# One PSUM bank in place of two for the scores whose maxima are taken, a fourth bank in the ring of the others, and a new order table

## The reference, cut to what matters

```python
# block 1 (L0), per window; block 2 (L1) adds rel_h and rel_w to the scores before the softmax
h = layer_norm(x, ln1_g, ln1_b)                  # then padded and cut into windows of 14 x 14
q, k, v = heads(h @ w_qkv.T + b_qkv)             # L0: q, k = rotated(q, k)
attn = softmax((q * hd ** -0.5) @ k.T)           # 12 heads
x = x + gamma_1 * ((attn @ v) @ w_proj.T + b_proj)
h = layer_norm(x, ln2_g, ln2_b)
x = x + gamma_2 * (gelu(h @ w_fc1.T + b_fc1) @ w_fc2.T + b_fc2)
```

## Time and profile before

| | |
|---|---|
| median of 3 runs | 572.3 us (570.03 to 575.05) |
| the profiled execution | 571.97 us, span 569.8 us from its first to its last instruction |
| PE busy | 521.0 us, 91% of the span |
| DVE busy | 386.6 us, 68% |
| ACT busy | 367.7 us, 65% |
| POOL busy | 226.7 us, 40% |
| mean granted clock of TensorE | 0.962 of full |

### The profile page before, as it was taken

One profiled execution on the slowest core, in us unless ns is written; L12 is line 12 of the kernel. 1 busy time (PEld: TensorE's weight loads), 2 busy tenths in 40 slices (PEclk: granted clock), 3 DMA queues, 4 the chain that ended last, 5 costly groups with the idle time before them and its releaser, 6 DMA issues.

```text
span 569.8 us, 13552 instructions
## 1 busy us (share of the span) xinstructions
PE 521.0 (91%) x4832; PEld 467.3 (82%) x4832; DVE 386.6 (68%) x915; ACT 367.7 (65%) x778; POOL 226.7 (40%) x324
## 2 busy tenths in 40 slices
PE   8767979999899999999999999999999999979875
PEld 7756868799798988888979898888889898868664
DVE  3887699968987758866758678776858677351230
ACT  0442347653959485969687886969688787755501
POOL 8233427625418353334536253343627234030210
PEclk9896699998999999999999999999999999988899
DMA  7410005000000000000000000000000000000000
GB/s 193 115 41 1 3 2 148 2 1 2 3 1 3 2 2 2 3 2 2 2 3 2 12 22 24 4 1 16 4 3 15 1 17 3 16 3 24 6 14 14
DMA packets 11055, 10.44 MB, mean 18 GB/s; under 512 B 3664, under 2 KB 9456, under 8 KB 10992
## 3 DMA queue, kind: packets, MB, share of 16 engines
q1 hardware_dynamic: 9264, 6.79, 4.5%
q10 hardware_dynamic: 1728, 2.81, 1.7%
HBM read 7.75 MB, written 1.57 MB: 16 GB/s over the span
## 4 chain that ended last, share of the span: by engine, by line
PE 57%; issue 17%; DVE 10%; POOL 7%; ACT 5%; DMA 2%; ACTq 0%; DVEq 0%; POOLq 0%
PE ps L1121 15%; PE ps L1324 9%; PE ps L1179 7%; PE ps L1193 5%; PE ps L1246 4%; PE ps L1269 4%; PE ps L1301 3%; DMA QT<-mT 2%; PE ps L1163 2%; PE ps L1219 1%; DVE mneg L713 1%; PE ps L1281 1%; PE ps L1208 1%; POOL QT L1041 1%; POOL xnm L353 1%
## 5 line engine op out<-in xcount | busy, mean ns | idle before, releaser
L882 ACT ACTIVATE PT<-ps 98x392 f32<-98x392 f32 x192 | 94.4, 496 | 52.7 <-PE ps L1246 51.6
L713 DVE TENSOR_REDUCE mneg<-ps 98x2 f32<-98x392 f32 x192 | 106.6, 560 | 32.1 <-PE ps L1193 29.9
L1246 PE MATMUL ps<-QT,KM 128*98 128x196 f32 x384 | 80.7, 293 | 3.1 <-DMA QT<-mT 2.4
L1193 PE MATMUL ps<-KM,QT 128*98 128x196 f32 x384 | 78.2, 286 | 3.6 <-DVE mneg L713 3.2
L1121 PE MATMUL ps<-WQ,XHa 128*128 128x384 f32 (+2 forms) x320 | 64.3, 305 | 5.4 <-DVE XHa L610 3.2
L1324 PE MATMUL ps<-W,GT 128*128 128x192 f32 x384 | 65.8, 328 | 2.6 <-ACT GT L924 2.5
L1121 PE MATMUL ps<-XHm,WF 128*128 128x256 f32 x384 | 64.6, 288 | 1.1 <-DVE XHm L610 1.0
L964 POOL TENSOR_SCALAR vepsm<-mvm 128x2 f32<-128x2 f32 x16 | 3.1, 193 | 155.8 <-DVE mvm L589 155.8
L1324 PEld LDWEIGHTS ps<-W,GT 128*128 128x128 f32 x384 | 62.0, 190 | 3.6 <-ACT GT L924 3.6
L812 ACT ACTIVATE KM<-ps 64x512 fp32r<-64x512 f32 x80 | 47.4, 592 | 24.7 <-PE ps L1179 24.2
L1193 PEld LDWEIGHTS ps<-KM,QT 128*98 128x98 f32 x384 | 52.2, 169 | 11.4 <-issue 4.0
(11 more groups left out here) (162 smaller groups left out, 1149.8 us busy)
## 6 DMA issues: line engine op xcount, KB each, us to landing
X<-in_x SPq DMA_DIRECT2D x8, 94.5 KB
out<-X SPq DMA_DIRECT2D x8, 94.5 KB
W<-in_w ACTq DMA_DIRECT2D x1, 576.0 KB, 5.6
W<-in_w SPq DMA_DIRECT2D x1, 576.0 KB, 3.9
raw<-in_w ACTq DMA_DIRECT2D x1, 384.0 KB, 3.5
raw<-in_w ACTq DMA_DIRECT2D x2, 192.0 KB, 4.2
raw<-in_w SPq DMA_DIRECT2D x1, 384.0 KB, 4.2
raw<-in_w SPq DMA_DIRECT2D x2, 192.0 KB, 4.8
```

The lines of the kernel that those rows point to most:

```text
L713: v.tensor_reduce(mneg[n % 2][0:CH, 0:2 * NH].rearrange("p (t h) -> p t h", t=2)[:, :, h], bank[0:CH, 0:2 * NM].rearrange("p (t k) -> p t ...
L882: a.activation(PT[:, at % (2 * GROUP), :], ps[0:CH, ST_BANK + h % 2, 0:2 * NM], ACT.Exp)\
L1193: last = mm(ps[0:CH, S_BANK + h % 2, NM * t:NM * t + NM], QT[p][:, h, CH * t:CH * t + CH], KM[p][:, h, 0:NM], start=True, stop=True)
L1246: last = mm(ps[0:CH, ST_BANK + h % 2, NM * c:NM * c + NM], KM[p][:, h, CH * c:CH * c + CH], QT[p][:, h, 0:NM], start=True, stop=True)
```

## The change

The scores use bank 0 alone, so `scores` of a head waits for the maxima of the head just before it. Bank 1 becomes `O_BANK`, and the ring has banks 4 to 7, four in place of three. All numbers of the calendar are new. The arithmetic stays as it is, and so do the numbers of instructions of each kind. The core of the diff:

```diff
-        S_BANK, ST_BANK, O_BANK, MISC, NMISC = 0, 2, 4, 5, 3
+        S_BANK, ST_BANK, O_BANK, MISC, NMISC = 0, 2, 1, 4, 4
...
-            {"et0": 4, "o1": 62, "k0": -73, "k2": -50, "qk0": -109, "dn": 105, "k1": -60, "v01": -87, "mx": 90,
...
+            {"mx": 90, "v01": -92, "et0": 12, "on": 66, "es0": -36, "q2": -54, "m": -9, "q1": -53, "es1": -31,
...
-        MOVES = {("prepare", 0): 1, ("attend", 15): -2, ("mlp", 2): 4, ("mlp", 14): 5, ("mlp", 1): 1,
...
+        MOVES = {("prepare", 0): 6, ("prepare", 1): 3, ("prepare", 7): 3, ("mlp", 14): 18, ("prepare", 5): 3,
...
-                bank = ps[:, S_BANK + h % 2, :]
+                bank = ps[:, S_BANK, :]
...
-                if NH * n + h >= 2:
-                    pe.wait_ge(e.mneg, NH * n + h - 1)
+                if NH * n + h >= 1:
+                    pe.wait_ge(e.mneg, NH * n + h)
                 for t in range(2):
-                    last = mm(ps[0:CH, S_BANK + h % 2, NM * t:NM * t + NM], QT[p][:, h, CH * t:CH * t + CH],
+                    last = mm(ps[0:CH, S_BANK, NM * t:NM * t + NM], QT[p][:, h, CH * t:CH * t + CH],
...
-                    mm(ps[:, S_BANK + 1, 0:128], ones[:], ones[:], start=True, stop=True)
+                    mm(ps[:, S_BANK, 0:128], ones[:], ones[:], start=True, stop=True)
```

More of the change, by code:

```diff
@@ L191, in build @@
         USES = (
[7 rows of a table removed]
[7 rows of a table added]
         )
         WORK = (
-            {"stats": -144, "inv_std": -140, "xn": -140, "xe": -134, "cosine": -96, "sine": -97, "rotate": -90,
[8 rows of a table removed]
-        )
-        ONCE = {"f0": 4, "wa": 99, "wb": 102, "f1": 134, "bk": 145}
-        SETUP = {"pads": -113, "bv0": -103, "values0": -92, "keys": -73, "scales0": 7, "fc00": 15, "fc01": 28,
-                 "scales1": 32, "lnb1": 91, "fc10": 100, "fc11": 131, "bare": 132, "values1": 149, "qkv1": 149,
-                 "clear": 152, "pads1": 163}
-        MOVES = {("prepare", 0): 1, ("attend", 15): -2, ("mlp", 2): 4, ("mlp", 14): 5, ("mlp", 1): 1,
-                 ("prepare", 1): -2, ("attend", 8): -1, ("mlp", 15): 2, ("prepare", 3): -1}
+            {"stats": -156, "inv_std": -148, "xn": -141, "xe": -138, "cosine": -102, "sine": -96,
[8 rows of a table added]
+        )
+        ONCE = {"f0": 16, "wa": 83, "wb": 104, "f1": 114, "bk": 169}
+        SETUP = {"pads": -107, "bv0": -104, "values0": -83, "keys": -79, "scales0": 12, "fc00": 15, "fc01": 30,
+                 "scales1": 50, "lnb1": 61, "fc10": 100, "fc11": 105, "bare": 110, "values1": 148, "qkv1": 155,
+                 "clear": 187, "pads1": 194}
+        MOVES = {("prepare", 0): 6, ("prepare", 1): 3, ("prepare", 7): 3, ("mlp", 14): 18, ("prepare", 5): 3,
+                 ("prepare", 6): 3, ("prepare", 2): 3, ("mlp", 1): 6, ("prepare", 3): 3, ("attend", 2): 2,
+                 ("prepare", 4): 3, ("attend", 3): 1, ("mlp", 0): 2, ("attend", 0): 1, ("mlp", 12): -1,
+                 ("attend", 15): -1, ("mlp", 2): 1, ("attend", 1): 1, ("attend", 14): -1, ("mlp", 9): -1,
+                 ("mlp", 6): -1, ("mlp", 4): -1, ("attend", 13): -1, ("attend", 4): 2, ("mlp", 13): -1,
+                 ("attend", 5): -1, ("mlp", 11): -1, ("mlp", 10): -1}
         CLOCK = {"fold": 28, ("qk0", 0): 10, ("x", 1): 20, ("mx", SLOTS - 1): 10, ("h0", SLOTS - 1): 5}
```

## The result

The changed kernel takes 551.14 us (median of 4 executions, 550.48 to 553.93) against 573.45 of the kernel before beside it. The ratio is 0.963, 95% interval 0.957 to 0.969: it is faster by 3.7%. I had said 566.0, with a range from 557 to 578; the direction was right and the size was not, the time lies under the range.

What follows compares the result with a forecast made beforehand. PE's own work was taken to bound the middle, handoffs the start and end. From 571.97 us, +1.5 +1.5 -3.9 -1.1 -2.4 = -4.4, then -1.7 for the clock, gave 565.9, stated as 566; range 557 to 578.

Steps and rivals of the forecast that it cites:

- One bank, the round trip: Between two heads' scores: 0.75 us of other PE work must lie there to cover the maxima.
- One bank, the price: Waits for maxima: +1.5 us in layer 0, +1.5 in slots 0 and 1, nothing in layer 1; bounds 0 and 52.8.
- The fourth ring bank: Mainly in the middle: waits for x's low part (2.7) and edge weights (1.2) go, -3.9 us; bounds 0 and -7.2.
- Rival (b): More gain: half-clock stretch goes whole, the middle gives its other 3.3 us or the start shortens; 556 us, chance 0.16.
- The end: After the last scores: handoffs covered by moved work, -2.4 us in sum; bounds +1.2 and -3.6.
- mx of slot 13: Near the end: its 1.14 us wait for tokens goes, with statistics 7 ticks earlier; -1.1 us.
- the clock: At 509.1 us: a 6.7 us half-clock stretch could give back 3.4 us; half of that taken, -1.7.
- The start: Reordered statistics and copies at the program's start: 0 change, within 2 us either way.
- The term for q0's read-out ahead of head 11's maxima: Layer 0: DVE reads out q0 before these maxima, costing 0.3 us in each of five slots, +1.5.
- (c): Gain paid back: the ring's 3.9 us is hidden or returns as other waits; 572 us, chance 0.22.
- (d): Slower: late DVE maxima stall PE in layer 0, slots 0 and 1, and layer 1's weight preparation; 581 us, chance 0.20.
- What would show it: Signs: maxima waits below 6 us, x's below 1, edge weights' gone, middle idle near 4; wrong if maxima waits reach 10.

Runs made afterwards that it cites:

- n_ring3: The changed kernel with three ring banks instead of four, still one bank for the scores; 579.4 us, ratio 1.009.
- o_clock13: The kernel before with five products of ones added ahead of mx of slot 13; 569.97 us, ratio 0.996.
- n_mlp14ones: The changed kernel with fc1 and fc2 of slot 14 moved back from 18 ticks late to 5, and 14 products of ones before mx of slot 14; 558.0 us.
- o_mlp14: The kernel before with fc1 and fc2 of slot 14 placed 18 ticks late instead of 5; 570.75 us, ratio 0.996.
- n_q0act5: The changed kernel with q0 of layer 0 read out by ACT instead of DVE, beside a repeat of the changed kernel; 551.11 us, ratio 0.964.

## Why the prediction was wrong, step by step

**One bank, the round trip.** 0.75 us estimated, 0.75 measured. Right.

**One bank, the price.** The old order would pay at most 52.8 us, I said, 64 heads late; measured, 23.6 in the old order (596.3 against 572.7). Less than half of the lateness became time: of the 19 us in slots 0 and 1, 4.6 did (52.1 against 47.5), and of the 33.8 behind them 22.3 (12.5, 7.7 and 2.1 in the next three columns), where PE is busy nearly all the time. For the new order I had +1.5 in layer 0, +1.5 in slots 0 and 1, nothing in layer 1. Measured on a ring of three: +3.0 to +5.6 in slots 0 and 1, +2.1 in slots 2 to 6, 0.0 in slots 7 to 14. The middle was exactly right (only slot 15 has a wait of 0.84 that I did not count), slots 2 to 6 nearly, slots 0 and 1 too small by 1.5 to 4: I took two full round trips there for two pairs of neighbouring heads, while DVE is busy 39.2 of 45.8 us and has something ahead of many of the other maxima too. It did not hurt the sum, because the order alone gave 4.7 us back in the same two slots. The Trainium skill's rule ("PSUM — Partial Sum Buffer", "Summary: rules for kernel authors", to write another bank than the one that is read) saves time where DVE is as loaded as PE, 3.0 to 5.6 us in two slots, and costs nothing to break in slots 7 to 14, where 0.75 us of other work lie between the scores.

**The fourth ring bank: the step that failed.** I took -3.9, with a bound of -7.2, "all idle time of the middle". The middle (slots 7 to 14) alone gave 9.8, or 8.2 like for like. Three things were wrong with it.

First, the bound: idle time in the view isn't all that PE waits. It was 254.50 - 247.26 = 7.24 us before and 244.70 - 242.05 = 2.65 after, so 4.6 us came from there. The other 5.2 came out of PE's *busy* time, 247.26 to 242.05. A part of that is work that only crossed the cuts. Before, the relative products of slot 8 began right behind the first scores of slot 7, where the stretch begins; now the first two stand ahead of these (which start at 228.02):
```profile
226.72 1.95 PE L1163 MATMUL ps<-Rbd,raw 96*128 96x348 f32 x6
```
```profile
225.25 0.77 PE L1167 MATMUL ps<-Rbd,raw 96*128 96x348 f32 x2
...
227.29 0.77 PE L1167 MATMUL ps<-Rbd,raw 96*128 96x348 f32 x2
```
Four matmuls at about 0.30 us from start to start, and four transposes of queries (0.36) that went behind the first scores of slot 15, are some 1.6 us. Some 3.6 us of busy time remain that were no work.

A matmul's end is modelled; where the next one waits, the one before is still shown at work, and only what is left counts as idle. The same two operations, in the same order, with and without a wait show how much: scores and then a relative product (g2) in slot 12, first in n_ring3, then in the changed kernel:
```profile
405.77 0.61 PE L1197 MATMUL ps<-KM,QT 128*98 128x196 f32 x2
406.64 0.82 PE L1167 MATMUL ps<-Rbd,raw 96*128 96x348 f32 x2 [0.26 <-DVE XHm L614]
```
```profile
383.79 0.61 PE L1197 MATMUL ps<-KM,QT 128*98 128x196 f32 x2
384.23 0.77 PE L1167 MATMUL ps<-Rbd,raw 96*128 96x348 f32 x2
```
From start to start it is 0.87 us against 0.44: 0.43 lost, 0.26 shown, 0.17 hidden. At two of the queries' transposes 0.63 was lost and 0.47 shown, 0.35 and 0.19; at dn and o1 0.24 and 0.08 each: about 0.16 hidden every time (at m, above, 0.07). The earlier trace rows had one such place, which I read only halfway: k2 starts 0.74 after scores that are shown as 0.61 long, so 0.13 is idle; the clean distance is not the 0.26 that I put there but 0.44, since these scores follow a relative product, so 0.30 was lost. The waits that I summed (2.7 for x in 4 places, 1.2 for edge weights in 5) thus cost some 1.5 us more than the view shows.

The clean comparison is n_ring3 against the changed kernel, with one order and the same matmuls in the middle:
```profile
239.50:499.40 259.90, 247.54 (x2381) 220.46 (x2381) 179.35 (x440) 201.89 (x439) 112.99 (x152) 1.00 0.03 7
```
Its 15.2 us more are 9.7 of idle time (12.36 against 2.65) and 5.5 of "busy". Counted in the two traces, PE has idle time before a matmul at 41 places of this stretch in n_ring3 and at 17 in the changed kernel. 24 places at 0.16 are 3.8 of the 5.5; the rest would be waits so short that the view shows none of them. From the kernel before (26 such places) to the changed one the same working gives only 1.4 of the 3.6; whether the other 2.2 were such short waits too, or come from the other neighbours that the same matmuls now have, isn't shown.

Second, the sum left waits out. Beside the 2.7 us for the low part of x, the view of before shows in the middle 1.8 us, in five places, in which PE's transposes wait for the low part of mx. I named them and added nothing for them. They fell to 0.3. Of the 1.2 for edge weights only 0.8 lay in the middle, and 0.6 of that stayed.

Third, and most of all, I costed the bank by the waits of the old order, as a part to be added. In the old order it is worth 1.6 us, even less than I took. What it is worth in the new one can't be read from the old trace: the new order stretches the time between filling and read-out of many banks (rows of n_ring3 above), and pays only with four: there the fourth bank is worth 24 to 27 us, 15.2 of them in the middle. Order and ring were one term, and I had them as two. Rival (b) named this direction ("the middle gives its other 3.3 us") at 0.16, but under the same wrong bound.

**The end.** -2.4 for handoffs, -1.1 for mx of slot 13 and -1.7 for the clock, -5.2 together; measured -10.3. The handoffs came off as told: dn, on, pr without idle time, 2.39 us of ones right ahead of mx of slot 15. Even mx of slot 14 behind the last weighted values came as told, with 0.83 us of wait at 521.26 (it was priced at +1.2). mx of slot 13 still waits 0.45 of its 1.14. The clock was mis-sized: I counted one stretch of 6.7 us and took half of what it gives back. Both stretches went, 10.2 us; o_clock13 measures 3.0 for them in the old end, net of its ones. That leaves some 7 us for handoffs where I had 3.5. n_mlp14ones puts 4.0 of these on the single move of slot 14's fc1 and fc2, where I had counted the idle rows that it removes; the hidden parts of those waits were again left out. In the old order the same move is worth 2.9 at most, clock included (o_mlp14). How the remaining 3 us or so divide among the other moves of the end was not measured.

**The start.** 0 within 2 us. The first scores start at 36.6 against 36.5. Right, though the slots behind it scatter by more than 4 us by themselves.

**Slots 2 to 6** lost 3.1 us where I had about 1.5; some 2.1 of that is work that came in over the cuts. The term for q0's read-out ahead of head 11's maxima was right in kind: PE waits for these at 0.33 us in slots 5 and 6, as I had put it, and at 0.82 in slot 2, not visibly in 3 and 4, and n_q0act5 takes the waits away. Its size in time isn't shown, since the 2.2 us of that profile go with another clock.

**The rivals.** (c), the gain is paid back, and (d), slower by DVE's lag, were wrong for this kernel; but (d) is what the same banks do in the old order, 594.7, with 39.4 us of waits for maxima. Its deciding point, order or no order, was the right one. **What would show it**: "waits for maxima below 6 us" was wrong (14.1, and above the 10 us that I had named as a sign of failure, as DVE's idle time at L717 was, 42.2 against 29.9) while the kernel was faster than forecast. The sign was badly chosen: it counts what one bank costs and nothing of what the ring and the order bring. Gone as told are the waits for the low part of x; the middle's idle time (2.65) is below the 4 that I named, and those for edge weights did not go.

## What to carry to other kernels

PE's idle time in a view is not a bound on what a better order can bring: compare start-to-start distances of the same operations with and without a wait; here a wait had mostly cost about 0.16 us more than was shown, and of the 15.2 us that the fourth ring bank saves in the middle 5.5 stood in the view as busy time. When two orders are compared over a stretch, count the work on both sides of the cuts first. Price a buffer together with the order that is to use it: here the bank was worth 1.6 us in the one and 24 to 27 in the other. Where a sequence at the end of a program has only handoffs, move a block of independent work into it, and count the clock too, since both low stretches went with the gaps.
